# A state-space and soft-expert layer on one core: one projection for the scores, two-bank VectorE instructions, an earlier first expert pair, and new turns

## The reference

```python
h = _layernorm(x) * (1 + ca) + sa                  # x: 8 batches x 256 tokens x 128
# state-space block: xn = rmsnorm(h); z, x_ssm, Bm, Cm, dt_raw = xn @ in_proj_w.T
# x_conv = silu(4-tap causal convolution of x_ssm); dt = softplus(dt_raw + dt_bias)
# h_t = h_(t-1) * exp(-exp(A_log) * dt_t) + dt_t * x_t (outer) B_t;  y_t = h_t . C_t + D * x_t
# out = h + (y * silu(z)) @ out_proj_w.T
x = x + ga * _L0_attn_ref(h, ...)
h = _layernorm(x) * (1 + cb) + sb
logits = jnp.einsum('bnd,esd->bnes', xn, sn)       # 8 experts x 64 slots
dispatch = jax.nn.softmax(logits, axis=1)          # over tokens
combine = jax.nn.softmax(logits.reshape(b, n, e * s), axis=-1)
slots = jnp.einsum('bnd,bnes->besd', xn, dispatch)
h = gelu(jnp.einsum('besd,edh->besh', slots, w1) + b1)   # 512 hidden
eo = jnp.einsum('besh,ehd->besd', h, w2) + b2
x = x + gb * jnp.einsum('bmd,bnm->bnd', eo, combine)
```

## Time and profile before

| what | value |
|---|---|
| median of 3 runs | 231.29 us (230.2 to 232.47) |
| span of the profiled execution | 227.2 us, 4247 instructions |
| TensorE, VectorE, ScalarE, GpSimd busy | 205.5, 139.5, 120.3, 60.9 us |

### The profile page before, as it was taken

One profiled execution on the slowest core, in us unless ns is written; L12 is line 12 of the kernel. 1 busy time (PEld: TensorE's weight loads), 2 busy tenths in 40 slices (PEclk: granted clock), 3 DMA queues, 4 the chain that ended last, 5 costly groups with the idle time before them and its releaser, 6 DMA issues.

```text
span 227.2 us, 4247 instructions
## 1 busy us (share of the span) xinstructions
PE 205.5 (90%) x1575; PEld 148.2 (65%) x1575; DVE 139.5 (61%) x372; ACT 120.3 (53%) x264; POOL 60.9 (27%) x147
## 2 busy tenths in 40 slices
PE   3879979995799899998978799989999999999995
PEld 2445555673377795475656387765865948659995
DVE  3887868998999956859988875730130221302753
ACT  3879896533468856797531566658327062270000
POOL 6545885016524203984015600000000000000000
PEclk9999999999999999999999999999999999999999
DMA  6404000200600000000500000006222141200122
GB/s 189 118 6 140 1 5 8 87 3 11 197 24 3 0 0 3 1 2 7 183 0 1 0 3 0 0 3 185 49 84 61 42 139 49 85 10 3 46 69 69
DMA packets 15344, 10.72 MB, mean 47 GB/s; under 512 B 1773, under 2 KB 13654, under 8 KB 15326
## 3 DMA queue, kind: packets, MB, share of 16 engines
q1 hardware_dynamic: 15100, 10.31, 15.5%
q10 hardware_dynamic: 226, 0.16, 0.2%
HBM read 9.34 MB, written 1.07 MB: 46 GB/s over the span
## 4 chain that ended last, share of the span: by engine, by line
PE 68%; DVE 11%; ACT 11%; POOL 4%; DMA 3%; issue 2%; ACTq 1%; DVEq 0%; POOLq 0%
PE bank L577 28%; PE bank L922 13%; PE bank L904 11%; PE bank L761 4%; PE bank L814 3%; PE bank L750 2%; POOL root L490 2%; DVE xcT L1309 2%; DVE bst L1183 2%; ACT zsT L1066 2%; PE bank L829 2%; DMA vec_nat<-ffn_slot_norm_gamma_dram 2%; ACT xhT L1072 1%; PE bank L835 1%; PE bank L860 1%
## 5 line engine op out<-in xcount | busy, mean ns | idle before, releaser
L1446 DVE TENSOR_TENSOR eo<-bank,seg_e 128x512 f32<-128x512 f32 x8 | 5.5, 692 | 47.9 <-PE bank L922 47.9
L922 PEld LDWEIGHTS bank<-w_sb,zsT 128*64 128x64 f32 x256 | 27.8, 137 | 3.0 <-issue 3.0
L922 PE MATMUL bank<-w_sb,xcT 128*64 128x128 f32 x256 | 28.8, 273 | 0.0
L922 PE MATMUL bank<-w_sb,zsT 128*64 128x128 f32 x256 | 28.8, 273 | 0.0
L922 PEld LDWEIGHTS bank<-w_sb,xcT 128*64 128x64 f32 x256 | 27.8, 137 | 0.0
L904 PE MATMUL bank<-slotsT,w_sb 128*128 128x512 f32 (+1 forms) x64 | 26.1, 558 | 0.2 <-ACT zsT L1140 0.2
L1140 ACT ACTIVATE zsT<-bank,vecT 128x512 f32<-128x512 f32 x16 | 10.7, 687 | 24.9 <-PE bank L904 24.9
L577 PE MATMUL bank<-xnT,winT 128*128 128x512 f32 x48 | 23.0, 607 | 0.3 <-ACT BT L1053 0.3
L490 POOL TENSOR_TENSOR root<-root,neg_half 128x2 f32<-128x2 f32 (+1 forms) x24 | 20.2, 842 | 2.0
L904 PEld LDWEIGHTS bank<-slotsT,w_sb 128*128 128x128 f32 x64 | 11.4, 190 | 12.6 <-issue 12.1
L1309 DVE SCALAR_TENSOR_TENSOR xcT<-bank,convw,xcT 128x510 f32<-128x510 f32 (+2 forms) x24 | 17.3, 737 | 3.6 <-ACT xcT L1050 3.3
(11 more groups left out here) (165 smaller groups left out, 414.9 us busy)
## 6 DMA issues: line engine op xcount, KB each, us to landing
w_sb<-in_L_ffn_w_dram SPq DMA_DIRECT2D x16, 256.0 KB, 2.9
mods_bc<-mod_dram SPq DMA_DIRECT2D x4, 320.0 KB, 3.5
xin<-in_L_attn_x_dram SPq DMA_DIRECT2D x4, 256.0 KB, 3.1
out_dram<-x1tok SPq DMA_DIRECT2D x16, 64.0 KB, 1.5
mods_bc<-mod_dram SPq DMA_DIRECT2D x4, 192.0 KB, 3.3
seg_e<-mod_dram SPq DMA_DIRECT2D x1, 512.0 KB, 3.8
eo<-in_L_attn_in_proj_w_dram SPq DMA_DIRECT2D x1, 384.0 KB, 4.1
eo<-in_L_wmod_dram SPq DMA_DIRECT2D x1, 256.0 KB, 4.6
```

The lines of the kernel that those rows point to most:

```text
L922: q = nc.tensor.matmul(o[j * S:(j + 1) * S, tile_cols(b)], act_h[j][k // 2][:, k % 2, at:at + S], w2_sb[j][:, k, :], start=k == 0 and b == ...
L1446: V.tensor_tensor(o, bank[4 + 2 * (it % 2) + g][:, :].rearrange("p (b d) -> p b d", d=P), b2_bc[:, it, :].unsqueeze(1).broadcast_to((P, 4, ...
```

## The change

One product M = Cᵀ-weights times B-weights is made at the start, and U = M xn takes the place of B and C: scores = xn times U. Four dt columns are appended to U (`dt_columns`), so that the score products give dt too; `dt_in` now reads `gm` and follows `copy_scores`. In `dt_times_x`, `token_max`, `slot_max` and `norm_slots` one VectorE instruction covers two banks or tiles (`slot_max`, `token_max` and `norm_slots` are rewritten like the one shown). The first expert pair is computed for six batches by `first_hidden`, `first_gelus`, `first_outputs`, and for the last two by `last_hidden`, `last_gelus`, `last_outputs`; w1 has a second pair of buffers. Every engine has a new table of turns. `rsm_rows(1)`, a ScalarE fill of the buffer that `send_parts` of A1 writes into, moves from turn 13 to turn 31, behind `copy_parts` of A1.

```diff
+            def dt_columns():
+                pool.wait_ge(s_act0, ACT_WIN)
+                for j in range(2):
+                    nc.gpsimd.tensor_copy(ut[j][:, :, L:L + H], winT[:, U0 + P:U0 + GB].unsqueeze(1).broadcast_to((P, BP, H))
+                                          ).then_inc(s_ut, 1)
...
-            visits = [((0, 2, 19, 20), var_root1), ((1, 4, 21, 22), ms_root1), ((5, 7, 23, 26), softplus),
-                      ((6, 8, 24, 27), add_basis), ((10, 9, 25, 28), gate_weights), ((11, 12, 29, 30), var_root(0)),
-                      ((13, 16, 31, 34), var_root(1)), ((14, 17, 32, 35), ms_root(0)), ((15, 18, 33, 36), ms_root(1))]
-            pipeline(pool, visits, once=[(3, slot_roots)])
+            visits = [((0, 2, 20, 21), var_root1), ((1, 5, 22, 23), ms_root1), ((6, 7, 24, 25), softplus),
+                      ((9, 8, 26, 27), add_basis), ((10, 11, 28, 29), gate_weights), ((12, 13, 30, 31), var_root(0)),
+                      ((14, 17, 32, 35), var_root(1)), ((15, 18, 33, 36), ms_root(0)), ((16, 19, 34, 37), ms_root(1))]
+            pipeline(pool, visits, once=[(3, dt_columns), (4, slot_roots)])
...
-            for n in range(ROW_BLOCKS):
-                q = nc.tensor.transpose(bank[1 + n // 4][:, tile_cols(n % 4)], w_nat[:, n, :], ident[:, :])
+            for n in range(2 * CT):
+                nc.tensor.transpose(bank[1][:, tile_cols(n)], w_nat[:, n, :], ident[:, :])
...
-                for t in range(TP):
-                    q = mm(b3[:, t * H:(t + 1) * H], xnT[j][:, tile_cols(t)], winT[:, DT0:ROWS])
-                q.then_inc(proj_ps[1][j], 1)
+                wait_before(pe, slotsT_done, j, it)
+                mm(b2[:, :], winT[:, U0:U0 + P], xnT[j][:, :]).then_inc(proj_ps[1][j], 1)
                 wait_before(pe, slots_done, j, it)
                 mm(b0[:, :], winT[:, X0:X0 + P], xnT[j][:, :]).then_inc(proj_ps[1][j], 1)
                 mm(b1[:, :], winT[:, X0 + P:X0 + 2 * P], xnT[j][:, :]).then_inc(proj_ps[1][j], 1)
-                wait_before(pe, slotsT_done, j, it)
-                mm(b2[:, :], winT[:, B0:B0 + P], xnT[j][:, :]).then_inc(proj_ps[1][j], 1)
+            def scores(j, it):
+                wait(pe, ut_done, j, it)
+                if it == 0:
+                    pe.wait_ge(s_ut, j + 1)
+                for bi in range(BP):
+                    o = bank[4 * j + 3 - bi]
+                    mm(o[:, 0:L + H], xnT[j][:, tile_cols(bi * NT)], ut[j][:, bi, :])
+                    mm(o[:, L + H:GW], xnT[j][:, tile_cols(bi * NT + 1)], ut[j][:, bi, P:L + H]).then_inc(g_ps[1][j], 1)
             def project2(j, it):
-                wait(pe, nabs_done, j, it)
-                mm(bank[4 * j + 3][:, :], winT[:, C0:C0 + P], xnT[j][:, :]).then_inc(proj_ps[1][j], 1)
-                wait(pe, xbc_done, j, it, 3)
-                mm(bank[4 * j + 2][:, :], winT[:, Z0:Z0 + P], xnT[j][:, :]).then_inc(z_ps[1][j], 1)
+                wait(pe, g_done, j, it, 1)
+                mm(bank[4 * j + 3][:, :], winT[:, Z0:Z0 + P], xnT[j][:, :]).then_inc(z_ps[1][j], 1)
             def project3(j, it):
-                wait(pe, xbc_done, j, it, 4)
-                mm(bank[4 * j + 3][:, :], winT[:, Z0 + P:Z0 + 2 * P], xnT[j][:, :]).then_inc(z_ps[1][j], 1)
-            def scores(j, it):
-                wait(pe, xbc_done, j, it)
-                for bi in range(BP):
-                    wait(pe, conv_done, j, it, bi + 1)
-                    o = bank[4 * j + bi]
-                    t0 = bi * L
-                    mm(o[:, 0:L], BT[j][:, t0:t0 + P], CTr[j][:, t0:t0 + L])
-                    mm(o[:, L:L + P], BT[j][:, t0 + P:t0 + L], CTr[j][:, t0 + P:t0 + L]).then_inc(g_ps[1][j], 1)
+                wait(pe, g_done, j, it, 2)
+                mm(bank[4 * j + 2][:, :], winT[:, Z0 + P:Z0 + 2 * P], xnT[j][:, :]).then_inc(z_ps[1][j], 1)
...
+            def first_hidden(e, half):
+                def visit():
+                    if e == 0 and half == 0:
+                        wait(pe, slotsT_done, 0, PASSES - 1)
+                        wait(pe, slotsT_done, 1, 0)
+                    wait(pe, w1_in[0], e, 0)
+                    for k in range(2 * half, 2 * half + 2):
+                        n = e * HC + k
+                        if n >= 2:
+                            pe.wait_ge(early_gelu, n - 1)
+                        nc.tensor.matmul(bank[n % 2][:, 0:EARLY * S], w1_sb[0][e][:, tile_cols(k)],
+                                         slotsT[:, e, 0:EARLY, :].rearrange("p b s -> p (b s)"),
+                                         start=True, stop=True, skip_group_check=True).then_inc(early_hid, 1)
+                return visit
+            def expert_out(o, k, b, at):
+                for j in range(2):
+                    q = nc.tensor.matmul(o[j * S:(j + 1) * S, tile_cols(at)],
+                                         act_h[j][k // 2][:, k % 2, b * S:(b + 1) * S], w2_sb[j][:, k, :],
+                                         start=k == 0 and at == 0, stop=k == HC - 1, skip_group_check=True)
+                return q
+            def first_outputs():
+                for j in range(2):
+                    wait(pe, w2_in, j, 0)
                 for k in range(HC):
-                    nc.tensor.matmul(bank[k][:, 0:EARLY * S], w1_sb[0][:, tile_cols(k)],
-                                     slotsT[:, 0, 0:EARLY, :].rearrange("p b s -> p (b s)"),
-                                     start=True, stop=False, skip_group_check=True)
+                    pe.wait_ge(early_gelu, HC + k + 1)
+                    for b in range(EARLY):
+                        expert_out(bank[2 + b // 4], k, b, b % 4)
+            pipeline(pe, visits, once=[(0, lambda: first_mods(1)), (1, mod_products), (4, t_wo), (5, t_slot_embeds),
+                                       (123, first_hidden(0, 0)),
+                                       (125, first_hidden(0, 1)), (126, first_hidden(1, 0)),
...
+            def last_hidden():
+                pe.wait_ge(early_gelu, 2 * HC)
+                for j in range(2):
+                    for k in range(HC):
+                        nc.tensor.matmul(bank[j][:, tile_cols(k)], w1_sb[0][j][:, tile_cols(k)],
+                                         slotsT[:, j, EARLY:, :].rearrange("p b s -> p (b s)"),
+                                         start=k == 0, stop=k == HC - 1, skip_group_check=True).then_inc(hid_ps[1][j], 1)
+            def last_outputs():
+                for k in range(HC):
+                    for j in range(2):
+                        wait(pe, gelu_done, j, 0, k + 1)
+                    for b in range(EARLY, B):
+                        q = expert_out(bank[3], k, b, b % 4)
+                q.then_inc(eo_ps, 2)
...
+            def copy_u(j, it):
+                wait(act, proj_ps, j, it, 1)
+                A(ut[j][:, :, 0:L], bank[4 * j + 2][:, :].rearrange("p (b t) -> p b t", b=BP), ACT.Identity,
+                  scale=vecT[:, RNW:RNW + 1]).then_inc(ut_done[1][j], 1)
...
-            visits = [((0, 6, 53, 56), mean_squares1), ((3, 12, 61, 65), copy_xnT), ((7, 14, 63, 68), exp_dt),
...
+            visits = [((0, 4, 52, 56), mean_squares1), ((3, 13, 61, 63), copy_xnT), ((12, 19, 68, 74), exp_dt),
+                      ((7, 17, 65, 72), first_tap), ((6, 15, 64, 71), copy_u), ((14, 23, 69, 78), silu_z(0)),
+                      ((16, 24, 70, 79), silu_z(1)), ((20, 25, 75, 80), silu_x(0)), ((21, 26, 76, 81), silu_x(1)),
+                      ((10, 18, 66, 73), copy_scores), ((22, 30, 77, 86), copy_parts), ((27, 35, 82, 89), decay(0)),
...
+            def first_gelus(e, half):
+                def visit():
+                    if e and half == 0:
+                        wait(act, y_ps, 1, PASSES - 1)
+                        wait(act, yg_done, 1, PASSES - 1)
+                    for k in range(2 * half, 2 * half + 2):
+                        n = e * HC + k
+                        act.wait_ge(early_hid, n + 1)
+                        A(act_h[e][k // 2][:, k % 2, 0:EARLY * S], bank[n % 2][:, 0:EARLY * S], ACT.Gelu,
+                          bias=b1_of(e, k)).then_inc(early_gelu, 1)
+                return visit
+            pipeline(act, visits, once=[(1, scale_win), (2, slot_squares), (5, unit_slots), (8, small_rows),
+                                        (9, copy_wo), (11, copy_sn), (31, lambda: rsm_rows(1).then_inc(s_act0, 1)),
+                                        (114, first_gelus(0, 0)),
+                                        (116, first_gelus(0, 1)), (117, first_gelus(1, 0)), (118, first_gelus(1, 1))])
...
             def dt_times_x(j, it):
-                for bi in range(BP):
-                    wait(dve, xht_ps, j, it, bi + 1)
-                    V.tensor_tensor(
-                        dtx[j][:, bi * NT:(bi + 1) * NT, :].rearrange("p t (h d) -> p (t h) d", h=H),
-                        bank[4 * j + bi][:, :].rearrange("p (g d) -> p g d", d=HD),
```

(41 more changed lines are left out.)

244 lines of the change are left out of this document (121 added, 123 removed).

## The result

The changed kernel takes 236.5 to 238.9 us; the ratio to the kernel before is 1.025, with a 95% interval of 1.018 to 1.032, so 5.8 us slower (4.2 to 7.5): slower beyond the noise, though not surely by 2%. The forecast of 235.1 in 227.5 to 238.8 holds it, and "slower" had the largest chance.

A forecast was written before the change was run, and what follows sets the result against it. Prediction: a pass is a ramp, a VectorE-bound stretch (`weigh`, `gate`, `x1`) and TensorE-bound routing. Terms +3.0 + 2.0 + 0.3 - 0.3 - 1.2 = +3.8 us gave span 231.0, time 235.1 us, range 227.5 to 238.8.

The forecast's parts named there:

- first cause: VectorE's `weigh` waits while GpSimd's long instructions run: +3.0 us in the second pass, +2.0 in the first.
- the move of the basis: GpSimd's basis and weights go behind both softplus chains, ten instructions and 8.2 us, where they meet `weigh`.
- the 6.7 us that I called worth nothing: Projection products and dt records taken off TensorE, 1.67 us a unit; in the ramp the scores eat the shorter work.
- The ramp: Second pass, first projection to first `weigh`: 20.3 us after the change, 20.1 before.
- The loads: Two more ScalarE table loads a pass, partly beside the wait for `dt_in`: 2.9 us come out as -0.3 at the decay.
- rival three: ScalarE has no cover for the loads: four times 1.43, 5.7 us more, 240.8 us; chance 0.06.
- The joins: One VectorE instruction over two banks saves a start, some 0.07 us, twice a pass in `dt_times_x`: -0.3 us.
- The first pair: First expert pair, last slot products to second pair: 18.2 us falls to 17.1 by filling TensorE's idle time, -1.2.
- The sum: Whole kernel: +3.0 + 2.0 + 0.3 - 0.3 - 1.2 = +3.8 us, span 231.0, time 235.1 us.
- the 5.0 for `weigh`: Delay of VectorE's `weigh` by GpSimd's long instructions over both passes, taken as reaching the end whole: 5.0 us.
- Rival one: No change: TensorE binds the VectorE stretches and the 5.0 us vanish in VectorE's slack; 230.1 us, chance 0.28.
- Rival two: Faster: the ramps really shorten, 3.3 us in the second and 1.3 in the first; 225.2 us, chance 0.22.

The follow-up runs named there:

- e2: Kernel before with only GpSimd's new turns (both softplus chains first, then basis and gated weights of both units): ratio 1.0067, 232.3 us.
- e5: e3's kernel with the second pass's GpSimd basis and gated weights of both units moved ahead of both softplus chains: ratio 1.0009, 231.2 us.
- e3: Changed kernel plus unread filler products in TensorE's three long waits of each pass: ratio 1.0057, 233.5 us.
- e9: Kernel before plus two unread filler products a pass, ahead of the first segment and the last output projection: ratio 0.9954, 230.7 us.
- e1: Changed kernel with GpSimd's turns put back as they were, first unit's basis and gated weights between the softplus chains: ratio 1.0500, 243.9 us.
- e4: Changed kernel with the exponential in the second unit's softplus replaced by a silu, two table loads less a pass: ratio 1.0203, 236.6 us.
- e8: e3's kernel with the exponential in the second unit's softplus replaced by a silu, two table loads less a pass: ratio 1.0105, 233.6 us.
- e10: e5's kernel with VectorE's two softplus instructions next to each other, no convolution step between: ratio 1.0006, 231.4 us.
- e12: e5's kernel with the joined VectorE instructions split again, one bank at a time: ratio 1.0037, 232.5 us.

## Why the prediction was right, and where not

- **The slower side and its first cause, right in kind, too large in size.** GpSimd's long instructions and `weigh` exclude each other (e2, e5). Forecast 3.0 us in the second pass; the traces of e3 and e5 show 2.2, the ratios 1.1. Forecast 2.0 in the first; in e3 the first three `weigh` take 2.95 against 2.84 before, and the next six some 5.0 against 3.8, so about 1.3. Up to the second pass e3 is 1.9 longer than the profiled execution of before, the shortest, and 0.8 longer than e9. Alone on the kernel before, the new turns cost 1.5 us for both passes (e2), where I had summed 5.0.
- **Its framing, wrong.** I priced the move of the basis against turns that the new order would have spoiled: leaving them costs 6 us more, a part of it through the clock (e1). The term is the price of the change, not of the move.
- **Missing: the clock.** The prediction never asked what TensorE does in the room of the 6.7 us that I called worth nothing. It is worth less than nothing: behind the waits that it leaves, the granted clock of the profiled execution is 0.50 for 10 us in each ramp and for 7 behind the first pass's last projection. In the compared executions, with some 14 to 20 us at the lower level, this costs 4.5 us (e3), 3.4 of it more than in the kernel before (e9).
- **The ramp, right.** First `weigh` 20.0 us after the first projection in e3 (forecast 20.3, before 20.1). At the falling clock it is 21.4.
- **The loads, right.** Four more stand in the trace and cost nothing that can be told from the noise (e4, e8); rival three is out, though the cover is thin (e10).
- **The joins, right within the error** (forecast 0.3, e12).
- **The first pair, wrong.** Forecast -1.2, measured +0.1 (18.3 against 18.2). TensorE's own work did not stay: eight early products and eight late ones take 1.29 + 3.10 + 1.46 + 2.05 = 7.9 us by the starts of their groups, before 2.58 + 1.05 + 3.60 = 7.2, and the idle time is 0.9 us (0.20 and 0.69), not the 0.4 that I left of 1.6. The 1.6 was wrong from the start: the trace of before shows 0.62 and 0.20 idle there; among others I had counted the eight hidden products at 6.9 instead of 7.2 and the slot products at 1.75 instead of 1.9. There was half as much to gain as I thought.
- **The sum, near by luck.** The forecast was 3.8 us over before, the measurement is 5.8. With the clock kept up it is 1.3 (e3), or 2.4 against e9, where the kernel before has its fillers too: my terms were too large by 1.4 to 2.5 us, mainly the 5.0 for `weigh`. The clock, for which I had no term, adds 4.5 (3.4 against e9). The two errors have opposite signs, and this is what keeps the time within the range.
- **Rival one:** without the clock the time would lie in its window (1.3 over before, e3). But its reason, slack in the VectorE stretches, is not what e5 shows: what VectorE loses there arrives whole. **Rival two** fell: no ramp is shorter by more than 0.9 us in any run.

## What to carry to other kernels

Before taking work off TensorE where it does not set the end, look at the waits that this leaves in its line: they can cost clock, and the products behind them pay; products that nobody reads, put into the wait, show whether it is so. When two engines exclude each other, place the long instructions of the one where the other has nothing that they stop (here the 12.8 us of idle GpSimd ahead of the softplus), and look again whenever the order around them changes.
